# A fused attention, ternary FFN, attention and FP8 FFN kernel: GpSimd normalises three of four probability tiles, the last products wait for their own weight pieces, and all queues are put in another order

## The reference

```
x = x + softmax((ctx Wq)(ctx Wk)^T) applied to layernorm(x)          # first attention
x = x + bitlinear(value * silu(gate)),  [value|gate] = bitlinear(rmsnorm(x))   # ternary FFN, hidden 1024
x = x + cross attention of layernorm(x) over ctx, 16 heads, 8 key/value heads  # second attention
x = x + (silu(x' G) * (x' U)) D with weights rounded to FP8 (e4m3), inner 768  # last FFN, x' = layernorm(x)
```

## Time and profile before

| | us |
|---|---|
| median of 3 runs (lowest, highest) | 319.15 (318.28, 320.42) |
| the profiled execution | 319.45 |
| its span, first to last instruction | 317.4 |
| PE busy | 294.9 (93%) |
| ACT busy | 258.5 (81%) |
| DVE busy | 252.2 (79%) |
| POOL busy | 217.9 (69%) |
| granted TensorE clock, mean | 0.993 of full speed |

### The profile page before, as it was taken

How to read it: one execution, slowest core, us unless ns; L and a number is a source line. 1 busy time by engine, 2 the same in 40 slices (tenths; PEclk the granted TensorE clock), 3 DMA queues, 4 the chain that set the end, 5 groups by cost and what they waited for, 6 DMA issues and landing times.

```text
span 317.4 us, 6401 instructions
## 1 busy us (share of the span) xinstructions
PE 294.9 (93%) x1981; PEld 258.8 (82%) x1992; DVE 252.2 (79%) x713; ACT 258.5 (81%) x607; POOL 217.9 (69%) x290
## 2 busy tenths in 40 slices
PE   3676999999999999999989999999999999999994
PEld 2465566889988987899779989889999998989784
DVE  3789698989888789888889788897877595766674
ACT  0869796489999989999997897788899998975350
POOL 3786663566887788797877897878897696772001
PEclk9999799999999999999999999999999999999999
DMA  7994602002046867678637566687665466200201
GB/s 219 380 350 135 176 0 68 1 1 76 5 81 179 245 168 199 165 209 202 180 88 207 150 179 162 165 221 203 147 188 151 116 197 200 69 2 0 68 1 66
DMA packets 54609, 44.59 MB, mean 140 GB/s; under 512 B 11696, under 2 KB 45104, under 8 KB 54576
## 3 DMA queue, kind: packets, MB, share of 16 engines
q1 hardware_dynamic: 54016, 43.93, 49.1%
q10 hardware_dynamic: 560, 0.26, 0.3%
HBM read 27.01 MB, written 15.20 MB: 133 GB/s over the span
## 4 chain that ended last, share of the span: by engine, by line
PE 21%; ACT 15%; POOL 8%; issue 5%; DVE 1%; ACTq 0%; POOLq 0%; DVEq 0%
PE pb L2015 14%; PE pb L2278 4%; ACT sm L980 4%; POOL tp_lo L666 4%; ACT pT_hi L992 3%; PE pb L2312 2%; POOL xn L588 1%; ACT sm L998 1%; ACT L980 1%; POOL sm L661 1%; ACT L1019 1%; ACT fuse L1019 1%; ACT q_hi L975 1%; ACT oT_hi L1004 1%; POOL rstd L582 1%
## 5 line engine op out<-in xcount | busy, mean ns | idle before, releaser
L666 POOL TENSOR_TENSOR tp_lo<-tp,pT_hi 128x512 fp32r<-128x512 f32 x54 | 69.2, 1297 | 20.9 <-ACT pT_hi L992 20.8
L980 ACT ACTIVATE sm<-sm,smin 128x256 f32<-128x256 f32 x128 | 63.6, 503 | 1.1 <-DVE smin L1563 0.7
L1563 DVE CUSTOM_DVE_ANT_0 sm<-pb,mask_all 128x256 f32<-128x256 f32 x128 | 47.5, 419 | 4.0 <-PE pb L2015 3.6
L1580 DVE STREAM_TRANSPOSE blocks<-sm 128x1024 f32<-128x1024 f32 x27 | 33.5, 1240 | 7.0 <-DMA block_room<-blocks 6.1
L2015 PE MATMUL pb<-ctx_hi,q_hi 128*128 128x256 f32 x128 | 37.8, 295 | 0.5 <-DVE q_lo L1550 0.4
L2015 PE MATMUL pb<-xT_hi,m_hi 128*128 128x256 f32 x128 | 37.2, 291 | 0.1
L2015 PE MATMUL pb<-n_hi,oT_hi 128*128 128x256 f32 x128 | 37.1, 290 | 0.1
L2015 PE MATMUL pb<-xT_hi,m_lo 128*128 128x256 f32 x128 | 36.2, 283 | 0.0
L2015 PE MATMUL pb<-xT_lo,m_hi 128*128 128x256 f32 x128 | 36.2, 283 | 0.0
L2015 PE MATMUL pb<-ctx_hi,q_lo 128*128 128x256 f32 x128 | 36.2, 282 | 0.0
L2015 PE MATMUL pb<-ctx_lo,q_hi 128*128 128x256 f32 x128 | 36.1, 282 | 0.0
(11 more groups left out here) (195 smaller groups left out, 946.4 us busy)
## 6 DMA issues: line engine op xcount, KB each, us to landing
block_room<-blocks SPq DMA_DIRECT2D x108, 128.0 KB, 2.5
tp<-block_room SPq DMA_DIRECT2D x54, 256.0 KB, 3.1
w_raw<-in_w SPq DMA_DIRECT2D x4, 576.0 KB, 4.2
wraw<-in_wgvT SPq DMA_DIRECT2D x4, 512.0 KB, 7.4
wraw<-in_woutT SPq DMA_DIRECT2D x2, 512.0 KB, 10.6
out<-xb SPq DMA_DIRECT2D x4, 256.0 KB, 2.2
xa<-in_x SPq DMA_DIRECT2D x3, 256.0 KB, 4.6
xb<-in_ctxT SPq DMA_DIRECT2D x2, 256.0 KB, 6.1
```

Source lines behind the costliest of these rows:

```text
L666: g.tensor_tensor(tp_lo[:, z, c, :], tp[:, z, c, :], as_f32(pT_hi[:, c, :]), ALU.subtract).then_inc(pT_lo_pool, 1)
L980: a.activation(sm[:, n % 2, k, :], sm[:, n % 2, k, :], ACT.Exp, bias=smin[:, n % 2, k:k + 1], scale=-1.0, accum_out=ssum[:, n % 2, k:k + 1 ...
L1563: v.tensor_tensor_reduce(out=sm[:, n % 2, k, :], in0=bank(passing_bank("s", 2 * n + h))[:, (k % 2) * S:(k % 2 + 1) * S], in1=mask_all[:, b ...
L1580: v.transpose(blocks[:].rearrange("p g k b -> p k g b"), sm[:, n % 2, :, :].rearrange("p k (g b) -> p k g b", b=32)).then_inc(blocks_done, 1)
```

## The change

1. POOL's `normalise` takes tiles 1, 2 and 3, ACT's only tile 0. The counts in `turn_blocks` and `probs4` follow.
2. `down(c, n)` of the first half waits for just as many FP8 pieces as reach its own rows of the down weights: 12, 13, 14, 15, 16 and 16 pieces for c = 0 to 5. Before, `down(0, 0)` waited for all 16.
3. The lists of all five queues and the bank list are written in another order.

```diff
@@ PASSING: the bank of each product in turn, all 40 lines differ
-        PASSING = [("project", 0, 4), ("context", 0, 2), ("xn", 0, 3), ("energy", 0, 4), ("project", 1, 5), ("xn", 1, 6),
+        PASSING = [("project", 0, 1), ("project", 1, 2), ("energy", 0, 6), ("energy", 1, 4), ("xn", 0, 0), ("project", 2, 5),
...
@@ sync
+            projection(0)
+            contexts(0)
             projection(1)
-            contexts(0)
-            projection(0)
             rows(1)
             rows(2)
+            gate_value(0)
+            contexts(1)
+            gate_value(1)
             rows(3)
-            gate_value(0)
             gate_value(2)
-            gate_value(1)
             gate_value(3)
-            contexts(1)
             hidden_out(0)
+            raw(6)
+            raw(2)
             raw(0)
+            hidden_out(1)
+            raw(1)
             norm_weight()
...
@@ gpsimd
             def normalise(n):
                 pool.wait_ge(srec_done, n + 1)
-                for k in (2, 3):
+                for k in range(1, 4):
                     g.tensor_scalar(sm[:, n % 2, k, :], sm[:, n % 2, k, :], srec[:, n % 2, k:k + 1], 1.0, ALU.mult, ALU.mult).then_inc(norm_done, 1)
...
@@ scalar
             def normalise(n):
                 act.wait_ge(srec_done, n + 1)
-                for k in (0, 1):
-                    a.activation(sm[:, n % 2, k, :], sm[:, n % 2, k, :], ACT.Identity, scale=srec[:, n % 2, k:k + 1]).then_inc(norm_act, 1)
+                a.activation(sm[:, n % 2, 0, :], sm[:, n % 2, 0, :], ACT.Identity, scale=srec[:, n % 2, 0:1]).then_inc(norm_act, 1)
...
@@ vector, turn_blocks (probs4 on tensor in the same way)
-                dve.wait_ge(norm_act, 2 * (n + 1))
-                dve.wait_ge(norm_done, 2 * (n + 1))
+                dve.wait_ge(norm_act, n + 1)
+                dve.wait_ge(norm_done, 3 * (n + 1))
...
@@ tensor
             def down(c, n):
                 h, i = divmod(c, KI)
                 pe.wait_ge(f_lo_done, c + 1)
+                if c < KI:
+                    pe.wait_ge(w8_done, -(-(2 * KD * INNER + (i + 1) * D) // PIECE))
                 if c == 0 and n == 0:
-                    pe.wait_ge(w8_done, B * EIGHTS)
```

More of the change, by code:

```diff
@@ new lines, in xattn_ffn_kernel @@
+        PASSING = [("project", 0, 1), ("project", 1, 2), ("energy", 0, 6), ("energy", 1, 4), ("xn", 0, 0), ("project", 2, 5),
+                   ("xn", 1, 6), ("probs", 0, 4), ("mean", 0, 2), ("mix", 0, 4), ("context", 0, 7), ("probs", 1, 0),
+                   ("project", 3, 5), ("energy", 2, 3), ("xn", 2, 7), ("xn", 3, 1), ("energy", 3, 6), ("mix", 1, 4),
+                   ("kv", 0, 3), ("kv", 1, 0), ("kv", 2, 2), ("hidden_in", 0, 5), ("kv", 3, 0), ("turn", 0, 2), ("probs", 2, 7),
+                   ("mean", 1, 1), ("value", 0, 5), ("gate", 0, 1), ("gate", 1, 3), ("value", 1, 6), ("value", 2, 0),
+                   ("mix", 2, 7), ("gate", 2, 1), ("vo", 0, 4), ("value", 3, 1), ("gate", 3, 6), ("gate", 4, 5), ("turn", 1, 6),
+                   ("vo", 1, 7), ("vo", 2, 4), ("value", 4, 1), ("vo", 3, 0), ("turn", 2, 2), ("qk", 0, 6), ("gate", 5, 7),
+                   ("gate", 6, 1), ("hidden", 0, 5), ("gate", 7, 7), ("hidden", 1, 0), ("qk", 1, 3), ("value", 5, 4),
+                   ("out", 0, 5), ("out", 1, 2), ("turn", 3, 0), ("probs", 3, 1), ("mix", 3, 5), ("turn", 4, 7), ("rows", 0, 2),
+                   ("vo", 4, 7), ("vo", 5, 1), ("q", 0, 4), ("vo", 6, 3), ("q", 1, 5), ("s", 0, 1), ("turn", 5, 4), ("s", 1, 2),
+                   ("context", 1, 0), ("turn", 6, 6), ("qk", 2, 4), ("s", 2, 6), ("value", 6, 5), ("value", 7, 7), ("s", 3, 3),
[4 rows of a table added]
+                   ("out", 3, 1), ("gate", 8, 2), ("gate", 9, 1), ("gate", 10, 5), ("q", 7, 3), ("s", 12, 5), ("s", 13, 1),
+                   ("rows", 1, 0), ("value", 8, 5), ("s", 14, 1), ("ctx", 3, 2), ("s", 15, 3), ("q", 8, 5), ("q", 9, 4),
+                   ("s", 16, 5), ("s", 17, 1), ("q", 10, 7), ("ctx", 4, 5), ("s", 18, 0), ("s", 19, 4), ("value", 9, 1),
+                   ("gate", 11, 4), ("ctx", 5, 3), ("value", 10, 7), ("value", 11, 5), ("s", 20, 1), ("ctx", 6, 1),
+                   ("s", 21, 0), ("q", 11, 2), ("q", 12, 4), ("s", 22, 3), ("ctx", 7, 7), ("s", 23, 2), ("q", 13, 0),
+                   ("ctx", 8, 1), ("s", 24, 4), ("s", 25, 3), ("gate", 12, 2), ("gate", 13, 4), ("q", 14, 5), ("s", 26, 0),
+                   ("s", 27, 7), ("ctx", 9, 4), ("out", 4, 3), ("gate", 14, 1), ("gate", 15, 0), ("out", 5, 3), ("s", 28, 7),
+                   ("s", 29, 0), ("value", 12, 3), ("q", 15, 2), ("ctx", 10, 5), ("s", 30, 3), ("value", 13, 2), ("ctx", 11, 0),
[16 rows of a table added]
@@ L697, in _ @@
             ternary_sum(0)
+            probs1(1)
             ternary_sum(1)
             ternary_sum(2)
-            probs1(1)
             base(0)
@@ L1029, in fuse_high @@
                 a.activation(f_hi[:, c % KI, :], fuse[:, c % KI, :], ACT.Copy).then_inc(f_hi_done, 1)
+            context_high(0)
             projected1(0)
-            context_high(0)
-            values_high(0)
-            rows1(0)
-            exps1(0)
             projected1(1)
             sums(0)
+            exps1(0)
+            exps1(1)
+            rows1(0)
             sums(1)
             probs1(0)
+            projected1(2)
             rows1(1)
-            exps1(1)
-            projected1(2)
+            values_high(0)
+            projected1(3)
+            sums(2)
             ternary(0)
             probs1(1)
-            projected1(3)
+            exps1(2)
             ternary(1)
-            exps1(2)
-            ternary(2)
-            sums(2)
-            rows1(2)
             turned_kv(0)
@@ L1053, in _ @@
             turned_kv(2)
+            ternary(2)
+            rows1(2)
             transposed(0)
+            rows1(3)
             ternary(3)
@@ L1061, in _ @@
             silu_direct(1, 0)
-            context_high(1)
+            silu_direct(1, 1)
+            silu_direct(2, 0)
             fused_outputs(0)
-            silu_direct(1, 1)
-            probs1(3)
-            rows1(3)
+            rounded(0)
             turned(0)
-            rounded(0)
+            fused_outputs(1)
             turned(1)
-            fused_outputs(1)
-            silu_direct(2, 0)
-            turned(2)
             fused_outputs(2)
@@ L1755, in _ @@
             masked(5, 1)
+            inverse(4)
+            q_low(6)
             second(2)
+            second(3)
+            outputs_low(1)
+            turn_blocks(4)
             inverse(5)
-            q_low(6)
-            second(3)
-            turn_blocks(4)
             third_stats(1)
             masked(6, 0)
-            outputs_low(2)
             masked(6, 1)
             q_low(7)
+            outputs_low(2)
             turn_blocks(5)
             eighths(2)
+            inverse(6)
             gated_half(4, 0)
+            masked(7, 0)
             third_low(1)
-            inverse(6)
-            masked(7, 0)
             masked(7, 1)
@@ L1853, in _ @@
             q_low(18)
+            u_scales(6)
             gated_half(7, 0)
+            inverse(17)
+            turn_blocks(16)
             eighths(8)
-            turn_blocks(16)
-            inverse(17)
             outputs_low(12)
@@ L2409, in _ @@
             scores(3, 1)
+            contexts(1, 0)
             queries(5)
-            contexts(1, 0)
             contexts(1, 1)
@@ L2538, in _ @@
             attn_out(13, 1)
+            contexts(15, 0)
             scores(20, 0)
-            scores(20, 1)
-            contexts(15, 0)
             contexts(15, 1)
             attn_out(14, 0)
+            scores(20, 1)
+            attn_out(14, 1)
             queries(22)
-            attn_out(14, 1)
+            ffn_out(6)
             contexts(16, 0)
```

791 lines of the change are left out of this document (387 added, 404 removed), and 46 rows, old and new, of the table PASSING.

## The result

The changed kernel takes **328.93 us** (median of 4 runs, 327.33 to 329.3), the kernel before beside it 319.78 (4 runs, 318.28 to 321.5): ratio 1.0274, 95% interval 1.0219 to 1.0329. It is 9 us slower.

What follows compares the result with a forecast made beforehand. PE, busy 93% of the span, was taken as the bound. 319.45 us - 2.2 (first stage) + 0 (third tile) + 0 (weight pieces and end) = 317.25, forecast as 317.0 because the profiled execution is 0.3 above the median; range 313.5 to 321.0.

Steps and rivals of the forecast that it cites:

- The fourth and third tile: 60 to 296 us: moving one more normalisation tile from ACT to POOL brings 0 us, bounds -4.66 and +7.6.
- (a): First stage: ACT's first table load comes before context_high(0), so energy(0) moves from 9.78 to about 9.2, 0.6 us.
- (d): First stage: five gate and value halves before mix(2); first SiLU 35.89 to 34.2, DVE's first multiplication 37.57 to 35.0.
- the first stage: PE's idle time from 5.3 to 40 us, 7.56 us: new order gains 2.2 us, bounds -7.56 and +1.5.
- (b): First stage: probs1(1) on POOL behind one ternary sum, not three; PE's turn at 21.91 about 2.5 us earlier.
- (c): First stage: ACT starts its list 2.5 us earlier and keeps 0.5, so the SiLU table is there at 34.2.
- Rival 2: First stage gives nothing: a DMA is late or ACT's list is through no earlier; 319.2 us, chance 0.18.
- Rival 1: POOL becomes the bound in its dense stretches and PE stalls for tp_lo; 324.6 us, chance 0.12.
- rival 4: SBUF contention lengthens POOL's normalisations; if all 96 took 987 ns, well above 325 us; chance 0.03.
- Rival 3: 60 to 296 us: ACT's relief removes half to all of PE's 4.66 us of stalls; 314.7 to 312.3, chance 0.25.
- The weight pieces and the end: Behind 296 us: finer waits for FP8 pieces only allow the new order; 0 us, bounds -0.5 and +1.
- The table loads: ACT's queue: 14 loads instead of 16, 2.6 us less, 5.3 with the skill page's drain; nothing in the sum.

Runs made afterwards that it cites:

- a_norm2: The changed kernel with the normalisation split as before, two tiles on ACT and two on POOL; 331.55 us, ratio 1.0392.
- a_read: The changed kernel with turn_hidden(7) ahead of both blocks_read(18) and eighth(3) on SyncE's list; 327.13 us, ratio 1.0188.
- a_late: a_read with eighth(3) moved from ahead of blocks_written(19) to directly ahead of blocks_read(20), as before the change; 323.74 us, ratio 1.0128.
- b_block: The kernel before with eighth(3) moved to directly ahead of blocks_written(19) on SyncE's list; 321.17 us, ratio 1.0057.
- h_first: The changed kernel up to fuse_qk(7), all five lists and the bank list behind it in the order of before; 319.65 us, ratio 1.0001.
- h_mid: The changed kernel up to about 160 us, all five lists and the bank list behind it in the order of before; 323.66 us, ratio 1.0119.
- a_swap: The changed kernel with turn_hidden(7) ahead of eighth(3) on SyncE's list, still behind blocks_read(18); 324.37 us, ratio 1.0175.
- a_rows: a_late with rows3(2) and third_low(2) moved up, placed as in the kernel before; 322.7 us, ratio 1.0091.
- a_fix: a_read with queries(15) moved up on ScalarE, directly behind silu(7) and ahead of exps(14, 0); 327.0 us, ratio 1.0228.
- a_sp: The changed kernel with SyncE's whole list behind turn_rows(1) as before, the other queues as changed; 326.25 us, ratio 1.0217.
- b_norm3: The kernel before with only the new normalisation split, three tiles on POOL and one on ACT; 317.92 us, ratio 0.9954.
- b_eighth: The kernel before with eighth(3) moved to directly ahead of turn_hidden(7) on SyncE's list; 319.86 us, ratio 1.0018.

## Why the prediction was wrong

**The step that failed** is the one that set the stretch of 60 to 296 us at 0 ("The fourth and third tile"). It asked only whether GpSimd could carry the third tile. It measured 8.7 us behind queries(3), and not by that cause: with two tiles on POOL (a_norm2) it is 12.6. What I had not costed is SyncE's list: eighth(3) had been moved ahead of turn_hidden(7) and of blocks_written(19). These 576 KB, directly ahead of a transfer that PE needs within a few microseconds, cost first 4.72 us of stall and about 1.9 us of slow products behind it (208.27 to 212.52 took 4.25 us; at the rate on either side I estimate 2.4 for the same products). With that mended by a_read, the same load costs 3.37 us through the block copies, turn_blocks(20) and added3(1), and again some slow products behind them (granted clock of 0.83 over 210 to 220). In the whole it is 6.5 us, shown from both sides: a_late takes all but 0.9 us of it away in the changed order, and b_block puts 2.3 us into the old one (1.5 us by the medians).

**The other 2.2 us**, up to queries(21), go with the order of the queues between fuse_qk(7) and 160 us: h_first, with the order of before from fuse_qk(7) on, has 109.8 us there, and h_mid, with the new order up to 160 us, has 112.4. Of the 2.2, 1.0 lie ahead of queries(11), where one and the same program spreads by 1.1, so whether they are a loss at all is open. The 1.2 behind it (0.9 in a_swap, a_read and a_late) stand clear of that spread. a_rows takes 0.7 of them away, which leaves it at 60.1 against 59.9 before, so a good part is the place of rows3(2), the turn of the third block of rows. a_fix took its stall away and gained nothing. Whether SyncE's order has a part in the 1.2 us is not shown: h_mid keeps the new order on all five queues, and a_sp, which has SyncE's old one, has a stall of its own there.

**(a) to (d), the first stage, -2.2.** Its signs came true in part, and the gain did not. PE and ACT, after:

```profile
8.73 3.17 PE L2055 MATMUL pb<-qk 128*128 128x256 f32 x8
...
32.92 2.31 PE L2089 MATMUL pb<-wgv,hqT 128*128 128x512 bf16 x9 [0.85 <-DVE wmean L1445]
```
```profile
2.19 1.28 ACT L869 ACT_TABLE_LOAD   x1 [2.19 <-issue]
...
34.50 1.28 ACT L945 ACT_TABLE_LOAD   x1
35.80 1.26 ACT L945 ACTIVATE wraw<-pb,gsc 128x512 f32<-128x512 f32 x2
```

energy(0) is at 8.73 (forecast 9.2) instead of 9.78, so (a) holds. (b) came out nearly so: PE turns the second batch's probabilities at 19.63 instead of 21.91. The norm weight landed at 12.83 + 11.0 = 23.8, as priced, and nothing waited for it. PE's first gate or value product is at 32.92 instead of 35.21 (I had wanted 32). But (c) fails: ACT reaches the SiLU table at 34.50, later than the 33.42 of the earlier trace rows, so that the wait of 1.19 us goes and 1.08 of it is lost again. The first SiLU is at 35.80, 0.1 us earlier than before, where I had 34.2, and DVE multiplies first at 36.52, where I had 35.0. The lead on PE was order, not time: the gate products had been moved ahead of other work. From the first of them to queries(3) all ten profiles with the new first stage take 44.2 to 44.4 us, and the four with the old one 41.9 to 42.5. At the common point nothing is left: queries(3) is at 78.1 us on the mean of those ten and at 78.0 on the mean of the four. These means mix granted clocks. The 0.6 us of the two profiles does too: before had 0.79 from 32 to 40 us, which I had expected to stay, and after has 1.00. Of the profiles with a clock of 1.00 all through to 40 us, the four with the new first stage reach queries(3) at 77.0 on the mean and the only one with the old (b_norm3) at 77.3. That is a lead of 0.3 us at best, where I had 2.2. In times there is no gain either: h_first and b_norm3, which differ in the first stage and the last waits alone, take 319.65 and 317.92.

**Rival 2** (the first stage gives nothing), to which I gave 0.18, was right for its part. **Rival 1** has the sign and over half the size (its 324.6 is 7.6 us above my sum, 5.4 above the kernel before; 9.2 was measured), but its cause is refuted: PE's waits for tp_lo are 0.4 us in all after the change, and the normalisations are no longer than in the earlier trace rows:

```profile
L661 POOL TENSOR_SCALAR sm<-sm,srec 128x256 f32<-128x256 f32 x96 | 44.9, 483 | 6.3 <-DVE srec L1568 6.2
```

That mean of 483 ns, against 488 before, also settles **rival 4**. The Trainium skill (GPSIMD Engine Reference, Specifications) says that GpSimd shares its SBUF interfaces with VectorE and that some of VectorE's instructions contend with it. That shows no price here with half as many of these instructions again. **Rival 3** (ACT's relief takes stalls away) is small in the old order: b_norm3 is 1.6 us faster by the medians, but by the profiles only 0.4 us of that lie behind queries(3). In the changed order the split is worth more, 2.6 us by the medians (a_norm2 against the changed kernel) and 3.9 by the profiles behind queries(3).

**The weight pieces and the end**, 0 us: right as a sum. Before and after, the last 102.6 us are the same to 0.1; the finer waits and the new order of the end were never taken apart, so that each alone is nothing is not shown.

**The table loads.** From a load's start to the next activation it is 35.80 - 34.50 = 1.30 us, and it is as much at 28 of the 30 loads of the two kernels; at the other two ACT waits for PE or for a DMA. The Trainium skill (ScalarE: Activation LUTs, What ACT_TABLE_LOAD costs) adds 1.38 us of drain to each switch; these traces show none.

**The range.** It failed because every case in it took the order of SyncE's list as neutral. The loss side of the middle was priced for GpSimd alone (+7.6, chance 0.12); a mechanism of its own for the moved DMAs, a transfer that is late by the few microseconds of a large load ahead of it, would have stood, by what a_read and the changed kernel show, at 319.45 + 4 to 7 us. Even that ends short of 328.93; the other 2.2 us of the middle come on top.

## What to carry to other kernels

When lists are reordered, go through the queue that issues the DMAs first: for each large load, look at which small transfer with a waiting consumer is issued less than a few microseconds behind it, and at how far ahead its consumer stands. The place on the list alone says little: b_eighth had the same neighbours without a loss. Compare two orders only at points ahead of which both hold the same work; an instruction that starts earlier because it was put earlier is no gain. A stall of about a microsecond on a full path may only move on when it is taken away (a_fix) or be gained for the most part (a_rows), so judge by common points and not by the one wait that went. Choose the points closely around the edit: over a longer stretch the spread between executions, here 1.1 us, hid a gain of 0.7.

## What the hardware showed that I had not expected

- A transposing DMA that took 3.1 to 3.4 us from issue to landing took 6.63 us when issued 0.53 us behind a load of 576 KB and 1.4 us behind two copies of 256 KB. With 2.95 us between the load and it (b_eighth) it took 3.5. Such a load is not the only thing that delays it: directly behind four block copies of 128 KB it took 4.95 (after, at 189.77) and 5.19 (a_swap, at 192.05), with no 576 KB near.
- After 4.72 us of idle time TensorE's products ran at 0.41 instead of 0.28 us until 212.5, with a granted clock of 0.83 over 200 to 220 (levels of 1.2 and 2.4 GHz). After the wait of 3.73 us in a_sp the eight products of ffn_out(5) likewise took 1.89 us; after 1.58 us in a_swap those of ffn_out(7) took 1.05.
- The first stage itself is not steady. With the same lists up to fuse_qk(7), four profiles have a clock of 1.00 from 5 to 20 us and reach queries(3) at 76.7 to 77.3 us, six have 0.83 to 0.89 and reach it at 78.4 to 79.4. The rows of after and of h_first for that stretch:

```profile
5.00:20.00 15.00, 12.48 (x49) 9.68 (x50) 10.50 (x33) 8.67 (x23) 10.47 (x18) 1.00 1.03 358
```
```profile
5.00:20.00 15.00, 11.72 (x41) 9.00 (x42) 9.37 (x31) 8.36 (x22) 10.28 (x18) 0.87 1.03 368
```

That is 1.9 us between executions on the mean, nearly the gain that I had forecast for this stage. What decides it no run here shows.
